# A fused decoder layer on one core: v projected from plain codes in four quarters, sine products swapped across partitions by transfers, and a new order of the four engines' lists

## The chip, the cores and the metric

The kernel runs on one core of one Trainium2 chip. The metric is device time in microseconds (us), the median of three runs. The engines are PE (TensorE, matrix products), DVE (VectorE), ACT (ScalarE), POOL (GpSimd) and SP (SyncE, which here only issues transfers). Each has its own list of instructions, written out by hand, and runs it in order; semaphores tie the lists together.

## What is computed

The reference takes x (128 sequences of 32 tokens, width 512) and computes, cut to what matters:

```
h = grouped_conv9(x) + context + bias
q, k, v = h @ Wq, h @ Wk, h @ Wv          # W = (codes - 8) * scale, one scale per 128 rows and column
q, k = rope(q), rope(k)                   # re = xe*cos - xo*sin ; ro = xo*cos + xe*sin
x = x + softmax(q k^T / sqrt(128) + causal) v @ Wo      # 32 query heads, 8 key/value heads of width 128
y = per-sequence 32x32 mixing of x (weights from a small network)
x = x + y @ Wbase^T + top-2-of-28 rank-8 LoRA experts(y)
```

## The kernel before

**Stages.** A setup block loads x, convolves it and leaves the hidden rows transposed in SBUF as two fp16 parts, high and low (`hT`). The attention block then runs 64 steps: 8 key/value heads (`g`) times 8 chunks of 512 tokens (`ch`). The last step runs into a tail that mixes the tokens and does the expert layer over 32 tiles of 128 tokens.

**A step.** Four query heads share one key/value head. Their projections fill PSUM banks 0 to 3 (`project_q(n, tile, kt)`), one matmul pair (high and low part of h) of 512 columns for each quarter `kt` of the width. The weights are plain codes, exact in fp16; between two quarters ACT multiplies the bank by a ratio of scales (`scale_q`), so that the sum ends in units of the last scale. The last scale is folded into the rope tables `rope_q` and `rope_k`. k does the same in bank 7 (`kv_bank`), scaled by DVE (`scale_k`). In the output projection ACT scales banks 4 and 5 (`scale_o`), and DVE adds the sum to `accT` (`add_out`).

v is different: its scales lie along the free axis. POOL multiplies its weights out once a head (`make_f`, `make_v_high`, `make_v_low`) and keeps a high and a low fp16 part. `project_v` therefore takes three passes (high by high, high by low, low by high) of four quarters for each of four token groups, 48 matmuls of 128 columns, in two halves; then ACT copies bank 7 to `v_f` (`move_v`) and POOL splits it (`v_high`, `v_low`).

**Rope.** DVE multiplies two banks at a time by the cosine (`turn_cos`, 128 partitions by 1024) and by the sine (`turn_sin`). The sine product of one half of the partitions belongs to the other half, so `turn_sin` writes across: two instructions of 64 partitions. POOL adds the two (`add_q`). Tiles 0 and 1 are pair 0, tiles 2 and 3 are pair 1. For k, POOL does all of it (`rotate_k_sin`, `rotate_k_cos`, `add_k`).

**Softmax.** `scores` makes 32 small matmuls onto the mask in bank 6; DVE transposes them and takes the maximum, POOL subtracts it (`shift`), ACT takes the exponential, DVE the sum and its inverse, POOL normalizes, DVE transposes back, POOL splits into two fp16 parts (`p_high`, `p_low`). `values` multiplies by v, and `out_high` (ACT) and `out_low` (DVE) split the result for the output projection.

**Pipeline.** One `body(n, i, p, r)` of each list works on four steps at once: the projections of n, the scores of i = n - 1, the values and most of the output of p = n - 2, and the end of the output of r = n - 3. Pair 0 of step n is turned at the end of body n; pair 1 is turned at the start of the next body, when it is step i. Before the change PE's body is: q(n,0,0), output(r,2,3), first half of v(i), q(n,0,1), values(p), second half of v(i), q(n,0,2), q(n,3,0), q(n,1,0), k(n,0), and then projections and output quarters in turn, with the scores in their midst. DVE's is: cosine of pair 1, add_out 2 and 3 of r, sine of pair 1, low halves 3, 1, 2, 0, mask, two scalings of k, scores transpose, maximum, third scaling of k, add_out 1 and 0, sum, inverse, cosine of pair 0 of n, transpose of the probabilities, sine of pair 0.

SP loads the codes of the next head in five pieces of 512 KB into two buffers, each when POOL has emptied one (`load_piece`), and the head's v scales.

Of the kernel before, what the change touches and what calls it, by code (L numbers as in the profile page):

```python
# [38 lines left out]
WSCALE = 256.0  # L39
# [11 lines left out]
class Rows:  # L51
# [28 lines left out]
class HeadWeights:  # L80
# [3 lines left out]
    def __init__(self, nc, c):  # L84
# [6 lines left out]
        self.k = sb("w_k", [P, 2, WKV // 2], F16)  # L91
        self.v = sb("w_v", [P, 2, 2, WKV // 2], F16)
# [3 lines left out]
        self.v_s = sb("v_s", [P, WKV // 2])  # L96
        self.f = sb("w_f", [P, WKV // 2])
# [10 lines left out]
        self.v_s_loaded = sem("v_s_loaded")  # L108
        self.piece_done = sem("piece_done")
        self.step = sem("w_step")  # L110

    def load_piece(self, sp, a, g, j):
# [7 lines left out]
        if j == 0:  # L120
            sp.dma_start(self.v_s[:], a["v_scales"][g].partition_broadcast(P)).then_inc(self.v_s_loaded, 16)
# [4 lines left out]
    def make_k(self, pool, g):  # L126
        self.wait_piece(pool, g, 0)
        pool.tensor_scalar(self.k[:, g % 2], self.codes[:, 0, 0:KT * HD], -8.0, 1.0, ALU.add, ALU.mult)

    def make_f(self, pool, g):  # L130
        pool.tensor_scalar(self.f[:], self.codes[:, 0, KT * HD:], -8.0, WSCALE, ALU.add, ALU.mult).then_inc(self.piece_done, 1)

    def make_v_high(self, pool, g):
        pool.wait_ge(self.v_s_loaded, 16 * (g + 1))
        pool.wait_ge(self.piece_done, PIECES * g + 1)
        pool.tensor_tensor(self.f[:], self.f[:], self.v_s[:], ALU.mult).then_inc(self.step, 1)
        pool.wait_ge(self.step, 2 * g + 1)
# [22 lines left out]
def prepare_and_convolve(nc, c, a, bank, accT, hT, w, rows):  # L160
# [39 lines left out]
    agg_hl = sb("agg_hl", [P, 2, S * S], F16)  # L200
    f_src = sb("f_src", [P, 2, 512])
# [28 lines left out]
    scale_step = sem("scale_step")  # L230
    conv_psum = sem("conv_psum")
# [26 lines left out]
    def _(sp):  # L258
# [51 lines left out]
    def _(pe):  # L310
# [61 lines left out]
        for n in range(2 * UNITS):  # L372
# [19 lines left out]
    def _(dve):  # L392
# [52 lines left out]

        def agg_lows(m):
# [16 lines left out]
        for n in range(2 * UNITS):  # L463
# [55 lines left out]
def attention_and_ffn(nc, c, a, banks, accT, hT, w, rows, out):  # L519
# [25 lines left out]
    q_sin = sb("q_sin", [P, 2, CHUNK])  # L545
    k_f = sb("k_f", [P, 2, CHUNK])
# [14 lines left out]
    v_psum = sem("v_psum")  # L561
    scores_psum = sem("scores_psum")
# [10 lines left out]
    q_sin_done = sems("q_sin_done", 2)  # L573
    q_ready = sems("q_ready", 2)
# [31 lines left out]
    lora = w.f[:, 0:2 * ER].rearrange("p (n e) -> p n e", n=2)  # L606
    loraT = w.v[0:EH, 0].rearrange("p a n -> p (a n)").rearrange("p (n l h t) -> p n l h t", n=2, l=2, h=2)
# [5 lines left out]
    gates = sb("gates", [P, 2, 2, EXPERTS])  # L613
# [79 lines left out]
    def _(sp):  # L693
        for g in range(1, NKV):
            for j in range(PIECES):
                w.load_piece(sp, a, g, j)


        def wait_chunk(ch):
# [4 lines left out]
            sp.wait_ge(v_psum, STEPS - CHUNKS + ch + 1)  # L704
# [10 lines left out]

        sp.dma_start(iota[:], a["iota"].partition_broadcast(P)).then_inc(iota_loaded, 16)
        wait_chunk(0)
        sp.dma_start(base, rows.base).then_inc(base_loaded, 16)
        wait_chunk(1)
        sp.dma_start(gl, rows.gl).then_inc(gl_loaded, 16)  # L720
        sp.dma_start(lb, rows.lb).then_inc(lb_loaded, 16)
        sp.wait_ge(mixw_zeroed, 2)
        for h in range(2):
# [3 lines left out]
        wait_chunk(5)  # L727
        sp.dma_start(aggb, rows.aggb.rearrange("b s -> (b s)").partition_broadcast(P)).then_inc(aggb_loaded, 16)
# [17 lines left out]
    def _(pe):  # L746
        def project_q(n, tile, kt):
            if kt:
                pe.wait_ge(q_scaled[tile], 3 * at(n) + kt)
            else:  # L750
                if n[1] == 0 and n[0]:
                    pe.wait_ge(w_ready, n[0])
                if at(n) and tile in (0, 3):

                    pe.wait_ge(q_sin_done[tile // 2], at(n))
                    pe.wait_ge(q_cos_done[tile // 2], at(n))
# [8 lines left out]
        def project_k(n, kt):  # L765
# [8 lines left out]
            for hp in range(2):  # L774
                mm = pe.matmul(kv_bank, w.k[:, n[2], kt * HD:(kt + 1) * HD], hT[:, n[1], kt, hp],  # L775
# [1001 lines left out]
```

## Time and profile before

| | |
|---|---|
| median of 3 runs (lowest, highest) | 1615.27 us (1615.13, 1615.29) |
| profiled execution: its time, its span | 1617.53 us, 1615.7 us |
| instructions | 36744 |
| PE busy | 1597.1 us, 99% |
| weight loads (overlap PE) | 894.6 us, 55% |
| DVE busy | 1399.0 us, 87% |
| ACT busy | 1231.1 us, 76% |
| POOL busy | 1127.9 us, 70% |
| transfers | 60.77 MB, 38 GB/s on average |
| granted TensorE clock | 0.997 |

The span is the profiled execution from its first to its last instruction. Busy time is a union over an engine's instructions; the ends of matmuls are modelled, and PE's pipelined matmuls overlap in it. An engine that waits in a semaphore is not busy. A mean duration of an instruction is longer than the time it takes of a full list where the next one starts before it has ended.

### The profile page before, as it was taken

What the parts mean: (1) busy time and instruction counts of PE and PEld (TensorE: products, weight loads), DVE (VectorE), ACT (ScalarE), POOL (GpSimd) and SP (SyncE); (2) the same over time, 40 slices, a digit from 0 to 9 for tenths busy, and PEclk for the clock granted to TensorE, in tenths of its full rate; (3) what the DMA queues carried; (4) which work ended last, traced back from release to release, by engine and by line L of the source; (5) the groups of instructions that cost most, each with busy time, mean ns of one, the idle gap of its engine ahead of it and who ended that gap; (6) DMA issues with size and microseconds to landing.
All of it is one profiled execution on the core that took longest, in us unless ns stands there. A gap on an engine that the chain in (4) does not pass through costs nothing.

```text
span 1615.7 us, 36744 instructions
## 1 busy us (share of the span) xinstructions
PE 1597.1 (99%) x14878; PEld 894.6 (55%) x14878; DVE 1399.0 (87%) x2176; ACT 1231.1 (76%) x2158; POOL 1127.9 (70%) x942
## 2 busy tenths in 40 slices
PE   9989999999999999999999999999999999899999
PEld 8845555555555555555555555555555555566665
DVE  5868888888888888888888888888888888888887
ACT  3458888888888888888888888888888888532222
POOL 1168877877787778777877787778787787623332
PEclk9999999999999999999999999999999999999999
DMA  8400010001000100010001000100000012122221
GB/s 303 136 25 15 14 34 15 14 15 34 15 14 14 34 14 15 14 34 14 14 15 34 14 15 15 34 14 15 15 2 28 26 11 83 34 72 80 79 82 50
DMA packets 32312, 60.77 MB, mean 38 GB/s; under 512 B 11512, under 2 KB 14392, under 8 KB 31888
## 3 DMA queue, kind: packets, MB, share of 16 engines
q1 hardware_dynamic: 32144, 58.42, 11.3%
q8 instruction: 119, 1.95, 0.5%
q14 instruction: 49, 0.40, 0.1%
HBM read 47.46 MB, written 10.95 MB: 36 GB/s over the span
## 4 chain that ended last, share of the span: by engine, by line
PE 92%; DVE 2%; POOL 1%; issue 0%; ACT 0%; POOLq 0%; DVEq 0%
PE banks L844 27%; PE banks L761 27%; PE banks L786 11%; PE banks L775 7%; PE banks L900 5%; PE banks L804 4%; PE banks L828 3%; PE banks L943 2%; PE banks L885 2%; PE banks L871 1%; PE banks L858 1%; POOL q_f L1408 1%; DVE q_sin L1136 0%; PE banks L934 0%; POOL k_f L1392 0%
## 5 line engine op out<-in xcount | busy, mean ns | idle before, releaser
L1530 ACT ACTIVATE banks<-banks,ratios 128x512 f32<-128x512 f32 x768 | 495.4, 676 | 119.9 <-PE banks L761 110.2
L761 PE MATMUL banks<-hT,w_q 128*128 128x512 f16 x2048 | 571.3, 380 | 7.4 <-DVE q_sin L1136 3.6
L844 PE MATMUL banks<-o_hl,w_o 128*128 128x512 f16 x2048 | 567.4, 379 | 0.6 <-DVE accT L1198 0.6
L1540 ACT ACTIVATE banks<-banks,ratios 128x512 f32<-128x512 f32 x768 | 479.4, 670 | 35.1 <-PE banks L844 35.0
L1408 POOL TENSOR_TENSOR q_f<-q_f,q_sin 128x1024 f32<-128x1024 f32 x128 | 301.7, 2357 | 68.6 <-DVE q_sin L1136 59.1
L844 PEld LDWEIGHTS banks<-o_hl,w_o 128*128 128x128 f16 x2048 | 187.0, 98 | 245.5 <-ACT banks L1540 50.4
L1136 DVE TENSOR_TENSOR q_sin<-banks,rope_q 64x1024 f32<-64x1024 f32 x256 | 312.8, 1222 | 8.1 <-POOL q_f L1408 2.4
L761 PEld LDWEIGHTS banks<-hT,w_q 128*128 128x128 f16 x2048 | 184.7, 98 | 236.0 <-DVE q_sin L1136 22.7
L786 PE MATMUL banks<-w_v,hT 128*128 128x128 f16 x3072 | 196.1, 221 | 0.0
L1129 DVE TENSOR_SCALAR banks<-banks,ratios 128x512 f32<-128x512 f32 x192 | 145.2, 756 | 56.7 <-PE banks L775 56.7
L786 PEld LDWEIGHTS banks<-w_v,hT 128*128 128x128 f16 x3072 | 180.1, 99 | 22.1 <-issue 0.7
L1392 POOL TENSOR_TENSOR k_f<-k_f,rope_k 64x512 f32<-64x512 f32 x128 | 162.3, 1268 | 14.5 <-POOL q_f L1408 10.7
L1198 DVE SCALAR_TENSOR_TENSOR accT<-banks,scales,accT 128x512 f32<-128x512 f32 x224 | 157.6, 745 | 9.4 <-PE banks L844 3.8
L1189 DVE TENSOR_TENSOR o_hl<-banks,o_hl 128x512 f16<-128x512 f32 x256 | 159.2, 684 | 2.9 <-ACT o_hl L1545 0.9
L1136 DVE TENSOR_TENSOR q_f<-banks,rope_q 128x1024 f32<-128x1024 f32 x128 | 154.1, 1204 | 3.6 <-PE banks L761 1.5
L775 PE MATMUL banks<-hT,w_k 128*128 128x512 f16 x512 | 152.8, 380 | 0.0
L1545 ACT ACTIVATE o_hl<-banks 128x512 f16<-128x512 f32 x256 | 132.3, 604 | 17.8 <-PE banks L828 17.8
L1412 POOL TENSOR_TENSOR sc<-sc,stats 128x512 f32<-128x512 f32 x64 | 67.0, 1047 | 103.3 <-DVE stats L1169 103.3
L1417 POOL TENSOR_TENSOR sc<-sc,stats 128x512 f32<-128x512 f32 x64 | 67.1, 1048 | 93.3 <-DVE stats L1177 93.3
L1156 DVE STREAM_TRANSPOSE sc<-banks 128x512 f32<-128x512 f32 x64 | 45.9, 717 | 74.4 <-PE banks L804 74.4
L1478 POOL TENSOR_TENSOR w_q<-hT,w_q 128x512 f16<-128x512 f32 x32 | 37.1, 1159 | 77.0 <-ACT w_q L1560 77.0
L900 PE MATMUL banks<-hT,w_o 128*128 128x512 f16 x372 | 85.4, 379 | 0.0
(131 smaller groups left out, 1930.0 us busy)
## 6 DMA issues: line engine op xcount, KB each, us to landing
codes<-in_codes SPq DMA_DIRECT2D x40, 512.0 KB, 3.7
accT<-in_xT SPq DMA_DIRECT2D x16, 512.0 KB, 9.7
hT<-in_x SPq DMA_DIRECT2D x32, 256.0 KB, 2.8
out<-codes SPq DMA_DIRECT2D x31, 256.0 KB, 2.0
v_s<-in_v_scales SPq DMA_DIRECT2D x8, 256.0 KB, 4.5
hT<-aggb_rows SPq DMA_DIRECT2D x1, 2048.0 KB, 7.1
f_src<-in_base_T SPq DMA_DIRECT2D x4, 256.0 KB, 9.6
base_rows<-f_hl SPq DMA_DIRECT2D x4, 256.0 KB, 3.2
```

The costliest lines, as they stand in the source:

```text
L761: mm = pe.matmul(banks[:, tile], w.q[:, n[2], kt * RF * HD + tile * HD:kt * RF * HD + (tile + 1) * HD], hT[:, n[1], kt, hp], start=kt == 0 ...
L775: mm = pe.matmul(kv_bank, w.k[:, n[2], kt * HD:(kt + 1) * HD], hT[:, n[1], kt, hp], start=kt == 0 and hp == 0, stop=hp == 1, skip_group_ch ...
L786: mm = pe.matmul(kv_bank[:, j * HD:(j + 1) * HD], hT[:, n[1], kt, hp, j * P:(j + 1) * P], w.v[:, n[2], wp, kt * HD:(kt + 1) * HD], start=m ...
L844: mm = pe.matmul(o_bank(tile), w.o[:, p[2], h * D + tile * P:h * D + (tile + 1) * P], o_hl[:, op, h], start=h == 0 and op == 0, stop=op == ...
L900: pe.matmul(base_bank(t), y_hl[:, t % 2, yp, k * P:(k + 1) * P], base[:, wp, k], start=i == 0, stop=False, skip_group_check=True)
L1136: return dve.tensor_tensor(dst.rearrange("p t (b s) -> p t b s", s=S), q, t, ALU.mult)
L1189: dve.tensor_tensor(lo, pv_bank(p, b).rearrange("p (j h q) -> p j h q", h=RF, q=S), hi, ALU.subtract).then_inc(out_ready[b], 1)
L1198: ins = dve.scalar_tensor_tensor(out=dst, in0=o_bank(tile), scalar=last, in1=dst, op0=ALU.mult, op1=ALU.add)
L1392: ins = pool.tensor_tensor(by_s(k_f[64 * h:64 * (h + 1), 1]), by_s(k_f[src, 0]), table(w.rope_k[:, n[2], 1], src), ALU.mult)
L1408: pool.tensor_tensor(q, q, q_sin[:], ALU.add).then_inc(q_ready[pair], 1)
L1530: act.activation(banks[:, tile], banks[:, tile], ACT.Copy, scale=w.ratios[:, n[0], tile, kt:kt + 1]).then_inc(q_scaled[tile], 1)
L1540: act.activation(o_bank(tile), o_bank(tile), ACT.Copy, scale=w.ratios[:, p[0], RF + tile, h:h + 1]).then_inc(o_scaled[tile], 1)
```

## The change

What it does, part by part:

- **v.** k and v now share one tensor of plain codes (`w.kv`), made by one POOL instruction a head. `project_v(n, kt)` does one quarter of the width at a time for all four token groups: 4 x 2 = 8 matmuls of 128 columns, 32 a step. After each quarter DVE multiplies bank 7 by a row of `v_table` (`scale_v`): the ratio of two scales, and after the last quarter the last scale, writing `v_f`. The table is made in the setup (six small DVE operations, one PE transpose, a store) and loaded once a head, broadcast over the partitions.
- **Sine.** `turn_sin` is one instruction of 128 partitions into `q_sin`. SP then issues two transfers of 64 partitions by 4 KB that put each half into the other half of a new buffer `q_sw` (`swap`), and `add_q` adds that. The sine waits until the previous swap has read `q_sin`, the swap until `add_q` of the other pair has read `q_sw`.
- **SP.** Its list is a body too: swap of pair 1 of i, loads of codes, table and tail data by chunk, swap of pair 0 of n.
- **Order.** Quarters 0 and 1 of v(n) lie at the end of body n, quarters 2 and 3 at the start of the next. Nothing of r is left in a body. New PE body: q(n,0,0), values(p), q(n,0,1), v(i,2), q(n,2,0), q(n,3,0), q(n,1,0), q(n,0,2), v(i,3), q(n,2,1), q(n,1,1), output(p,0,0), output(p,1,0), k(n,0), output(p,0,1), q(n,3,1), output(p,1,1), k(n,1), output(p,0,2), scores(i), output(p,1,2), output(p,0,3), k(n,2), q(n,1,2), output(p,1,3), q(n,0,3), output(p,2,0), k(n,3), q(n,1,3), output(p,3,0), output(p,2,1), v(n,0), output(p,3,1), q(n,2,2), output(p,2,2), v(n,1), output(p,3,2), q(n,3,2), output(p,2,3), output(p,3,3), q(n,2,3), q(n,3,3).
- New DVE body: cosine and sine of pair 1 of i, low half 3, scale_v(i,2), low halves 0, 2, 1, scale_v(i,3), mask, scale_k 0 and 1, scores transpose, maximum, add_out(p,0), scale_k 2, add_out(p,1), sum, inverse, sine of pair 0 of n, scale_v(n,0), cosine of pair 0, transpose of the probabilities, scale_v(n,1), add_out(p,2), add_out(p,3).
- New POOL body: rotate_k_cos(i), add_k(i), add_q(i,1), v_high, v_low, dequantize, shift, normalize, rotate_k_sin(n), p_high, p_low, add_q(n,0). ACT loses `move_v` and follows PE's new order.

The core of the diff:

```diff
+        def swap(n, pair):
+            sp.wait_ge(q_sin_done[pair], at(n) + 1)
+            if pair or at(n):
+                sp.wait_ge(q_ready[1 - pair], at(n) + pair)
+            for h in range(2):
+                sp.dma_start(q_sw[64 * h:64 * (h + 1)], q_sin[64 * (1 - h):64 * (2 - h)]).then_inc(q_swapped[pair], 16)
...
+        def load_weights(i):
+            g, ch, _ = i
+            if g + 1 < NKV:
+                if ch in (1, 3, 4):
+                    w.load_piece(sp, a, g + 1, {1: 2, 3: 3, 4: 4}[ch])
+                if ch == 2:
+                    if g:
+                        sp.wait_ge(v_moved, CHUNKS * g)
+                    w.load_v_table(sp, rows, g + 1)
+            if g + 2 < NKV and ch in (5, 6):
+                w.load_piece(sp, a, g + 2, 6 - ch)
...
-        def project_v(n, half):
-            if half == 0:
+        def project_v(n, kt):
+            if kt:
+                pe.wait_ge(v_scaled, 3 * at(n) + kt)
+            else:
                 pe.wait_ge(k_moved, at(n) + 1)
-            for j in (2 * half, 2 * half + 1):
-                m = 0
-                for kt in range(KT):
-                    for hp, wp in PASSES:
-                        mm = pe.matmul(kv_bank[:, j * HD:(j + 1) * HD], hT[:, n[1], kt, hp, j * P:(j + 1) * P],
-                                       w.v[:, n[2], wp, kt * HD:(kt + 1) * HD], start=m == 0, stop=m == 3 * KT - 1)
-                        m += 1
-            if half:
-                mm.then_inc(v_psum, 1)
+            for j in range(CT):
+                for hp in range(2):
+                    mm = pe.matmul(kv_bank[:, j * HD:(j + 1) * HD], hT[:, n[1], kt, hp, j * P:(j + 1) * P],
+                                   w.kv[:, n[2], (KT + kt) * HD:(KT + kt + 1) * HD], start=kt == 0 and j == 0 and hp == 0,
+                                   stop=hp == 1, skip_group_check=True)
+            mm.then_inc(v_psum, 1)
...
         def turn_sin(n, pair):
+            wait_q(n, pair)
             if pair or at(n):
-                dve.wait_ge(q_ready[1 - pair], at(n) + pair)
-            for h in range(2):
-                ins = turn(n, pair, 1, slice(64 * (1 - h), 64 * (2 - h)), q_sin[64 * h:64 * (h + 1)])
-            ins.then_inc(q_sin_done[pair], 1)
+                dve.wait_ge(q_swapped[1 - pair], 32 * (at(n) + pair))
+            turn(n, pair, 1, q_sin[:]).then_inc(q_sin_done[pair], 1)
+
+        def scale_v(n, kt):
+            dve.wait_ge(v_psum, KT * at(n) + kt + 1)
+            if n[1] == 0 and kt == 0:
+                dve.wait_ge(w.v_table_loaded, 16 * (n[0] + 1))
+            v = kv_bank.rearrange("p (j d) -> p j d", d=HD)
+            table = w.v_table[:, n[2], kt].unsqueeze(1).broadcast_to([P, CT, HD])
+            if kt < KT - 1:
+                dve.tensor_tensor(v, v, table, ALU.mult).then_inc(v_scaled, 1)
+            else:
+                if at(n):
+                    dve.wait_ge(v_ready, at(n))
+                dve.tensor_tensor(v_f[:], v, table, ALU.mult).then_inc(v_moved, 1)
...
         def add_q(n, pair):
-            pool.wait_ge(q_sin_done[pair], at(n) + 1)
-            if pair:
-                pool.wait_ge(k_sin_done, at(n) + 1)
+            pool.wait_ge(q_swapped[pair], 32 * (at(n) + 1))
+            pool.wait_ge(q_cos_done[pair], at(n) + 1)
+            if at(n) == 0 and pair == 0:
+                pool.wait_ge(k_sin_done, 1)
             q = q_f[:, 2 * pair:2 * pair + 2]
-            pool.tensor_tensor(q, q, q_sin[:], ALU.add).then_inc(q_ready[pair], 1)
+            pool.tensor_tensor(q, q, q_sw[:], ALU.add).then_inc(q_ready[pair], 1)
```

## Rows read from the trace of the kernel before

**Rows 1.** One line's instructions: ACT's move of k, once a step.

```profile
L1536 ACT ACTIVATE k_f<-banks x64: 589/628/634, 84.0 to 1375.6; 128x512 f32<-128x512 f32 x64
```

**Rows 2.** Groups by line and form: line, engine, tiles, forms, count | busy us, mean ns | idle before.

```profile
L1530 ACT ACTIVATE banks<-banks,ratios 128x512 f32<-128x512 f32 x768 | 495.4, 676 | 119.9 <-PE banks L761 110.2
...
L1136 DVE TENSOR_TENSOR q_sin<-banks,rope_q 64x1024 f32<-64x1024 f32 x256 | 312.8, 1222 | 8.1 <-POOL q_f L1408 2.4
L1408 POOL TENSOR_TENSOR q_f<-q_f,q_sin 128x1024 f32<-128x1024 f32 x128 | 301.7, 2357 | 68.6 <-DVE q_sin L1136 59.1 <-POOL k_f L1392 0.4
...
L1392 POOL TENSOR_TENSOR k_f<-k_f,rope_k 64x512 f32<-64x512 f32 x128 | 162.3, 1268 | 14.5 <-POOL q_f L1408 10.7
...
L1129 DVE TENSOR_SCALAR banks<-banks,ratios 128x512 f32<-128x512 f32 x192 | 145.2, 756 | 56.7 <-PE banks L775 56.7
...
L1440 POOL TENSOR_TENSOR pT_hl<-pT,pT_hl 128x512 f16<-128x512 f32 x64 | 74.0, 1156 | 5.1
...
L1417 POOL TENSOR_TENSOR sc<-sc,stats 128x512 f32<-128x512 f32 x64 | 67.1, 1048 | 93.3 <-DVE stats L1177 93.3
...
L1425 POOL CAST pT_hl<-pT 128x512 f16<-128x512 f32 x64 | 38.9, 608 | 0.0
```

**Rows 3.** Timeline of PE in one step: start, length, engine, line, tiles, count.

```profile
703.99 0.85 PE L828 MATMUL banks<-pT_hl,v_hl 32*128 32x128 f16 x48
...
704.78 1.51 PE L786 MATMUL banks<-w_v,hT 128*128 128x128 f16 x24
...
706.13 1.51 PE L761 MATMUL banks<-hT,w_q 128*128 128x512 f16 x6
...
711.57 1.08 PE L804 MATMUL banks<-q_f,k_f 128*32 128x128 f32 x32
...
712.59 1.04 PE L844 MATMUL banks<-o_hl,w_o 128*128 128x512 f16 x4
...
713.46 0.59 PE L775 MATMUL banks<-hT,w_k 128*128 128x512 f16 x2
```

**Rows 4.** The same timeline, DVE's instructions.

```profile
701.23 1.23 DVE L1136 TENSOR_TENSOR q_f<-banks,rope_q 128x1024 f32<-128x1024 f32 x1
...
702.37 1.40 DVE L1198 SCALAR_TENSOR_TENSOR accT<-banks,scales,accT 128x512 f32<-128x512 f32 x2
...
706.29 2.48 DVE L1189 TENSOR_TENSOR o_hl<-banks,o_hl 128x512 f16<-128x512 f32 x4
...
708.69 0.68 DVE L1165 CAST banks<-mask_b 128x512 f32<-128x512 bf16 x1
...
712.72 0.72 DVE L1156 STREAM_TRANSPOSE sc<-banks 128x512 f32<-128x512 f32 x1 [1.14 <-PE banks L804]
...
713.47 0.69 DVE L1169 TENSOR_REDUCE stats<-sc 128x16 f32<-128x512 f32 x1
...
714.96 1.41 DVE L1198 SCALAR_TENSOR_TENSOR accT<-banks,scales,accT 128x512 f32<-128x512 f32 x2
...
716.28 0.68 DVE L1173 TENSOR_REDUCE stats<-sc 128x16 f32<-128x512 f32 x1
...
717.16 1.18 DVE L1136 TENSOR_TENSOR q_f<-banks,rope_q 128x1024 f32<-128x1024 f32 x1
...
721.63 1.23 DVE L1136 TENSOR_TENSOR q_f<-banks,rope_q 128x1024 f32<-128x1024 f32 x1
```

**Rows 5.** Transfers by issue: tiles, queue, count, KB each, median us to landing.

```profile
codes<-in_codes SPq DMA_DIRECT2D x40, 512.0 KB, 3.7
...
out<-codes SPq DMA_DIRECT2D x31, 256.0 KB, 2.0
v_s<-in_v_scales SPq DMA_DIRECT2D x8, 256.0 KB, 4.5
```

**Rows 6.** Timeline of SP in the tail: two issues one behind the other.

```profile
1502.54 0.34 SPq L714 DMA_DIRECT2D out<-codes  x1
1502.92 0.43 SPq L710 DMA_DIRECT2D hT<-in_x  x1
```

More of the change, by code:

```diff
@@ L726, in _, with body @@
                              rows.aggw[:, h].rearrange("(t b) (i o) -> b i t o", b=TB, i=S)[b]).then_inc(mixw_loaded, 16)
-        wait_chunk(5)
-        sp.dma_start(aggb, rows.aggb.rearrange("b s -> (b s)").partition_broadcast(P)).then_inc(aggb_loaded, 16)
+        w.load_v_table(sp, rows, 0)
+        for j in range(2):
+            w.load_piece(sp, a, 1, j)
+        def body(n, i, p, r):
+            if i:
+                swap(i, 1)
+            if i:
+                load_weights(i)
+                load_ffn(i)
+            if n:
+                swap(n, 0)
+        swap(FIRST, 0)
+        program(body)
+        swap(LAST, 1)
         wait_chunk(6)
@@ L836, in output @@
             else:
-                if tile == (1 if p not in (PRIOR, LAST) else 0):
-                    for b in (0, 2, 1, 3):
+                if tile == 0:
+                    for b in (1, 2, 0, 3):
                         pe.wait_ge(out_ready[b], at(p) + 1)
@@ L979, in body @@
                 output(p, 1, 2)
-                output(p, 0, 2)
+                output(p, 0, 3)
             if n:
@@ L996, in body @@
             if n:
-                project_q(n, 2, 2)
+                project_k(n, 3)
+                project_q(n, 1, 3)
+            if p:
+                output(p, 3, 0)
+                output(p, 2, 1)
+            if n:
+                project_v(n, 0)
             if p:
@@ L1129, in scale_k, with turn, wait_q @@
             dve.tensor_scalar(kv_bank, kv_bank, w.ratios[:, n[0], K_ROW, kt:kt + 1], None, ALU.mult).then_inc(k_scaled, 1)
[L1131 to L1135 removed]
+        def turn(n, pair, which, dst):
+            t = w.rope_q[:, n[2], which, 2 * pair:2 * pair + 2].unsqueeze(2).broadcast_to([P, 2, CHUNK // S, S])
+            q = banks[:, 2 * pair:2 * pair + 2].rearrange("p t (b s) -> p t b s", s=S)
             return dve.tensor_tensor(dst.rearrange("p t (b s) -> p t b s", s=S), q, t, ALU.mult)
[L1138 to L1139 removed]
+        def wait_q(n, pair):
+            for tile in ((1, 0), (3, 2))[pair]:
                 dve.wait_ge(q_psum[tile], KT * at(n) + KT)
@@ L1287, in body @@
                 softmax_max(i)
+            if p:
+                add_out(p, 0)
             if n:
@@ L1296, in body @@
             if n:
+                turn_sin(n, 0)
+                scale_v(n, 0)
                 turn_cos(n, 0)
@@ L1300, in body @@
             if n:
-                turn_sin(n, 0)
+                scale_v(n, 1)
+            if p:
+                add_out(p, 2)
+                add_out(p, 3)
         scale_k(FIRST, 0)
```

335 lines of the change are left out of this document (176 added, 159 removed).

## The prediction

> **What bounds the kernel now.** I read the busy shares of the page first (the table above): PE 99%, DVE 87%, ACT 76%, POOL 70%. Such shares are averages, and PE's matmul ends are modelled, so I went on to one step of the attention loop. The row of line 1536 gives the beat: 64 steps, from 84.0 to 1375.6 us [rows 1], 20.5 us apart on average; the steady beat is that of DVE's cosine product, from 701.23 to 721.63, 20.4 us [rows 4]. So some 1265 of 1615.7 us are 62 equal beats, and the change is worth 62 times what it does to one.
>
> What PE does in a beat, from its timeline [rows 3]: between 712.59 and 713.46 four 512-column matmuls start, so a pair (one projection or output quarter) takes 0.432; 24 matmuls of v take 706.13 - 704.78 = 1.35, or 0.056 each; the values 704.78 - 703.99 = 0.79; the scores 712.59 - 711.57 = 1.02. A step has 36 pairs (16 of q, 4 of k, 16 of the output), 48 v matmuls, values, scores: 15.55 + 2.70 + 0.79 + 1.02 = 20.06. PE thus loses only 0.35 of 20.41 to waiting.
>
> DVE's timeline [rows 4] shows that it is bound too, in one half of the beat. From the transpose of the scores at 712.72 (1.15 after their first matmul) to the next cosine product at 721.63 it hardly pauses: 8.9 us; from 701.23 to the scores at 711.57 it is PE's list that runs out, 10.34 us. 10.34 + 1.15 + 8.91 = 20.40. The two halves meet in both engines, so a gain on one comes through only as far as the other allows. That is the sum to make for the new order.
>
> **The change on PE.** v takes plain codes, two passes instead of three: 32 matmuls of 128 columns for 48. 16 x 0.056 = 0.90 us a step goes; a quarter (8 matmuls) takes 0.45. PE's work is 19.16 a step.
>
> **The change on DVE.** Each sine product is two instructions of 64 partitions, 1222 ns each [rows 2]. One of 128 partitions is the shape of the cosine product: 1.23 long, and the next instruction starts 702.37 - 701.23 = 1.14 later [rows 4]. Twice a step, 4 x 1.22 - 2 x 1.14 = 2.60 goes. Four scalings of v by the table come, 128x512, PSUM times SBUF. The trace has no such instruction. Nearest below: the low halves of the output (PSUM and SBUF in, 128x512), four in 708.69 - 706.29, 0.60 each [rows 4]; nearest above: k's scaling, PSUM to PSUM, 0.756 [rows 2], with no overlap into the next. I take 0.60, since the 0.756 has a scale read per partition, which here is not there. So +2.40, between 2.40 and 3.02. DVE's total hardly moves; what counts is where it lies.
>
> **The beat of the new order.** Let S be the first matmul of scores(i). DVE's half, by starts [rows 4]: transpose at 1.15, +0.75 (713.47 - 712.72) maximum, +0.62 (its 0.69 less the usual overlap) add_out(0) at 2.52, +0.66 (716.28 - 714.96, halved) scale_k at 3.18, +0.67 add_out(1) at 3.85, +0.66 sum at 4.51, +0.88 (717.16 - 716.28, sum and inverse) sine of n at 5.39, +1.14 scale_v at 6.53, +0.60 cosine at 7.13, +1.14 transpose of the probabilities at 8.27, +0.72 scale_v at 8.99, +0.60 and twice 0.66, next cosine at 10.91. Against 10.06 (1.15 + 8.91) before: two scalings and both add_out of tiles 2 and 3 now lie in this half, one half sine less.
>
> PE's list in that half is the scores, 20 pairs, 2 quarters of v: 1.02 + 8.64 + 0.90 = 10.56, and its last q pair starts at 10.13. A pair ends 0.59 after its start [rows 3], a hop between engines costs about 0.06 (711.57 + 1.08 to 712.72, rows 3 and 4 together), so the cosine may start at 10.78, plus some 0.1 lost where ACT's scaling (0.676, [rows 2]) of an output tile has only three pairs of cover: 10.9. Both engines arrive together.
>
> The other half: the next cosine 1.14, its sine 1.23 to the end, hop 0.06: at 2.43 the banks of tiles 2 and 3 come free and PE, which has done q(0,0), the values, q(0,1) and a quarter of v by 2.1 after its own start, has waited some 0.4. From there 14 pairs and one quarter to the scores: 6.05 + 0.45 = 6.50. Around output(0,0), which waits for low halves 3, a v scaling, 0, 2, 1 behind the sine (2.38 + 5 x 0.60 + 0.08 + 0.06 = 5.5 against PE's 5.47), and at output(0,1) another 0.1. Half: 9.03. Beat: 10.91 + 9.03 = 19.94; I take 19.97, as three more things arrive within 0.1 of their need.
>
> One of them is POOL. k's sine halves, 2 x 1.27, now stand between normalize (1.05) and p_high (0.61), p_low (1.16) [rows 2]. Inverse ends 5.47, normalize 6.6, k's sine 9.2, p_low 11.06; the values of the next body start at 11.1. No slack, no loss.
>
> **The transfers.** Each sine product crosses the partitions by two transfers of 256 KB from SP. SP's issues stand 1502.92 - 1502.54 = 0.38 apart, 0.43 long [rows 6]; a 256 KB store out of SBUF lands 2.0 after its issue, a 512 KB load 3.7 [rows 5]. So both land after 0.4 + 2.0 = 2.4 at least, 0.4 + 3.7 = 4.1 at most; I take 2.7, nearer the store, since source and size are its own. Pair 1: sine ends at 2.4 after the cosine; add_q(n,0) on POOL, which frees the buffer, ends about then (11.06 + 2.36 = 13.4 after S, cosine at 10.9); hop, 2.7, add_q 2.36 [rows 2], hop: 7.8 against scores at 9.0. k_cos and add_k (two of 1.27) are done meanwhile. Cover 1.2: it holds to a landing of 3.9. Pair 0's has more. Codes and the v table are queued on SP behind the swap of pair 1, one a step, and nothing ahead of it waits: every wait of load_weights is for work of an earlier body.
>
> The trace's store and load bracket the landing with no rule needed. The Trainium skill ("DMA: Bandwidth & Descriptors", Anatomy of one DMA) gives about 2.0 us fixed, most of it the write's receipt, plus bytes over 436 GB/s, fitted on GpSimd's path; by it the 512 KB of a swap take an estimated 3.2 us. The sum would be the same 19.97 with 0.7 us of cover left in place of 1.2; it speaks for the slow case below, not for another likeliest one.
>
> **Other parts.** POOL's v weights (f, high, low) go, once a head, off the path: nothing. ACT loses one 0.6 copy: nothing, it idles. The v table in the setup: six small DVE operations, one transpose, one store of 16 KB under PE's convolution; if uncovered, under 2 us once. Before the last step's scores the same shorter lists apply: about -1.
>
> **Sum.** (20.41 - 19.97) x 62 = 27; with the end, -28. The profiled execution was 1617.5 with a span of 1615.7, 2.3 over the median of 1615.27; by medians 1587.
>
> **Rivals.** (1) PE alone sets the beat: the DVE half shrinks (its operations overlap better, or PE's wait for the sine is filled): 20.41 - 0.90 = 19.51, 1559. For: PE waits 0.35 only today. Against: the 10.91 above leaves it no room. (2) The scalings cost 0.756 without overlap, sines 1.22: 2 x 0.16 + 0.1 in DVE's half, 0.16 + 0.1 in the other's chain of low halves: +0.6 at most, beat 20.2 to 20.5, 1602 to 1621, most likely 1612: gains eaten. For: PSUM to PSUM is the dearer form in the trace. (3) Slower, by one mechanism: the swap lands late. Over 3.9 each microsecond is one on the beat; break-even at 3.9 + 0.44 = 4.35; at 5.0 the beat is 21.1 and the time 1655. For: the v scales' 256 KB took 4.5 behind a load [rows 5], and every step has two swaps. Against: the store's 2.0. (4) PE never notices v at all because DVE still sets 20.4: excluded by the shorter first half, save through (2).
>
> **How the numbers follow.** Forecast 0.53 (1579 to 1597); (1) 0.10; (2) 0.20; (3) 0.15; anything else 0.02. Below 1568 I leave some 0.05, over 1618 0.15 of (3) and a little of (2): range 1568 to 1618. A change under 0.2% (3.2 us) cannot be told. Faster: 0.53 + 0.10 + 0.13 of (2) = 0.77; same 0.06; slower 0.17.
>
> **What would show it.** The beat (line of k's move) at 19.9 to 20.0; 32 v matmuls a step at 0.056; the sine at about 1.2 for 128x1024, starting 1.14 behind the cosine; v's scaling under 0.70; q_sw landing 2.4 to 3.2 after the first issue, and scores not waiting for POOL's q_f; a PE wait of about 0.4 on q_sin and DVE without a gap from the scores' transpose to the cosine. It is wrong if scores wait for q_f (3), if a v scaling shows 0.75 (2), or if DVE has gaps in that half (1).

## The result and the profile after

The new kernel takes 1639.07 us (four runs, 1638.68 to 1639.18) against 1615.28 (1615.13 to 1616.33): a ratio of 1.0145, interval 1.0128 to 1.0163. It is slower by 23.8 us, where 28 less was forecast. The profiled execution took 1639.18 with a span of 1637.4, so the terms below are made against the forecast's span, 1615.7 - 28 = 1587.7: a miss of 49.7.

The first lines of the page after. Every engine is busy for less time than before, in a longer span:

```profile
span 1637.4 us, 35390 instructions
...
PE 1581.3 (97%) x13854; PEld 837.4 (51%) x13855; DVE 1373.0 (84%) x2311; ACT 1209.4 (74%) x2094; POOL 1105.3 (68%) x910
```

The line of k's move, after, answers to [rows 1]. 63 distances, 20.70 on average, where before had 20.50:

```profile
L1632 ACT ACTIVATE k_f<-banks x64: 578/587/597, 84.6 to 1388.4; 128x512 f32<-128x512 f32 x64
```

They aren't all alike. Of the first 62 distances from one step's scores to the next, 28 lie between 20.55 and 20.8, 20 are shorter, down to 20.34, and 14 are longer, up to 21.6. A step like the one shown next takes 20.69 to 20.70, which is called the steady beat below.

The groups by line and form, after, answer to [rows 2]. The operations came out as priced; the new thing is what stands at the end of the first line:

```profile
L1506 POOL TENSOR_TENSOR q_f<-q_f,q_sw 128x1024 f32<-128x1024 f32 x128 | 301.1, 2352 | 127.3 <-DMA q_sw<-q_sin 127.3
...
L1209 DVE TENSOR_TENSOR q_sin<-banks,rope_q 128x1024 f32<-128x1024 f32 x128 | 152.6, 1193 | 2.0 <-PE banks L829 1.4 <-DMA q_sw<-q_sin 0.6
...
L1236 DVE TENSOR_TENSOR banks<-banks,v_table 128x512 f32<-128x512 f32 x192 | 130.9, 682 | 2.0 <-PE banks L854 2.0
```

The waits of all engines, after (us in total, times, longest): `add_q` waits for the swap, and the scores' weight loads wait for `add_q`.

```profile
POOL q_f L1506 <- DMA q_sw<-q_sin: 127.3, 70, 2.9
...
PEld banks L871 <- POOL q_f L1506: 39.6, 62, 1.6
```

One step in the timeline, after. DVE, answering to [rows 4]: the transpose of one step's scores, the cosine and sine of pair 1, the transpose of the next step's scores.

```profile
700.02 0.72 DVE L1244 STREAM_TRANSPOSE sc<-banks 128x512 f32<-128x512 f32 x1 [0.83 <-PE banks L871]
...
709.81 1.23 DVE L1209 TENSOR_TENSOR q_f<-banks,rope_q 128x1024 f32<-128x1024 f32 x1
710.95 1.22 DVE L1209 TENSOR_TENSOR q_sin<-banks,rope_q 128x1024 f32<-128x1024 f32 x1
...
720.72 0.72 DVE L1244 STREAM_TRANSPOSE sc<-banks 128x512 f32<-128x512 f32 x1 [0.84 <-PE banks L871]
```

PE, answering to [rows 3]: the values with a wait ahead of them, and the scores.

```profile
708.75 1.46 PE L829 MATMUL banks<-hT,w_q 128*128 128x512 f16 x6
710.60 0.85 PE L896 MATMUL banks<-pT_hl,v_hl 32*128 32x128 f16 x48 [0.40 <-issue]
...
718.92 0.59 PE L912 MATMUL banks<-o_hl,w_o 128*128 128x512 f16 x2
719.57 1.08 PE L871 MATMUL banks<-q_f,k_f 128*32 128x128 f32 x32
```

POOL, from the dequantizing of codes (L132) and shift (L1510) over normalize (L1515) to `add_q(i,1)`:

```profile
700.70 1.04 POOL L132 TENSOR_SCALAR w_o<-codes 128x1024 f16<-128x1024 int32 x1
701.82 1.05 POOL L1510 TENSOR_TENSOR sc<-sc,stats 128x512 f32<-128x512 f32 x1
704.62 1.05 POOL L1515 TENSOR_TENSOR sc<-sc,stats 128x512 f32<-128x512 f32 x1 [1.75 <-DVE stats L1265]
705.84 2.59 POOL L1489 TENSOR_TENSOR k_f<-k_f,rope_k 64x512 f32<-64x512 f32 x2 [0.17 <-POOL sc L1515]
708.55 0.61 POOL L1525 CAST pT_hl<-pT 128x512 f16<-128x512 f32 x1
709.24 1.16 POOL L1540 TENSOR_TENSOR pT_hl<-pT,pT_hl 128x512 f16<-128x512 f32 x1
710.35 2.36 POOL L1506 TENSOR_TENSOR q_f<-q_f,q_sw 128x1024 f32<-128x1024 f32 x1
...
714.02 1.26 POOL L1498 TENSOR_TENSOR k_f<-k_f 128x512 f32<-128x512 f32 x1
717.17 2.35 POOL L1506 TENSOR_TENSOR q_f<-q_f,q_sw 128x1024 f32<-128x1024 f32 x1 [1.89 <-DMA q_sw<-q_sin]
```

SP in that step:

```profile
712.78 1.10 SPq L740 DMA_DIRECT2D q_sw<-q_sin  x2
```

**The chain in these rows.** Pair 1's sine ends at 710.95 + 1.22 = 712.17. The buffer `q_sw` is free only when `add_q` of pair 0 ends, at 710.35 + 2.36 = 712.71; SP issues at 712.78. `add_q(i,1)` starts at 717.17, 4.39 after the issue, ends at 719.52, and the scores start at 719.57. POOL has been idle for 1.89, as k's `add_k` was done at 715.28. From cosine to scores: 719.57 - 709.81 = 9.76, against a forecast of 9.03. The other half came as forecast: scores start 1.15 ahead of their transpose, so at 698.87, and 709.81 - 698.87 = 10.94 against 10.91. 10.94 + 9.76 = 20.70.

### The profile page after: what moved, and what is told of

Its sections match the earlier page's. It is cut to its first block and busy times, and to the rows that moved or that the text cites. A ratio compares the mean times of both kernels' runs of the same rounds, so it can differ in the third digit from the quotient of the medians.

```text
span 1637.4 us, 35390 instructions
## 1 busy us (share of the span) xinstructions
PE 1581.3 (97%) x13854; PEld 837.4 (51%) x13855; DVE 1373.0 (84%) x2311; ACT 1209.4 (74%) x2094; POOL 1105.3 (68%) x910
## 5 line engine op out<-in xcount | busy, mean ns | idle before, releaser
L1506 POOL TENSOR_TENSOR q_f<-q_f,q_sw 128x1024 f32<-128x1024 f32 x128 | 301.1, 2352 | 127.3 <-DMA q_sw<-q_sin 127.3
L829 PEld LDWEIGHTS banks<-hT,w_q 128*128 128x128 f16 x2048 | 175.5, 97 | 249.6 <-ACT banks L1626 67.7
L912 PEld LDWEIGHTS banks<-o_hl,w_o 128*128 128x128 f16 x2048 | 176.5, 98 | 238.4 <-ACT banks L1636 73.0
L854 PEld LDWEIGHTS banks<-w_kv,hT 128*128 128x128 f16 x2048 | 133.4, 98 | 67.4 <-ACT k_f L1632 14.5
L854 PE MATMUL banks<-w_kv,hT 128*128 128x128 f16 x2048 | 157.4, 220 | 2.5 <-DVE banks L1236 2.0
L1209 DVE TENSOR_TENSOR q_sin<-banks,rope_q 128x1024 f32<-128x1024 f32 x128 | 152.6, 1193 | 2.0 <-PE banks L829 1.4
L843 PE MATMUL banks<-hT,w_kv 128*128 128x512 f16 x512 | 152.3, 379 | 1.2 <-DVE banks L1203 1.2
L1515 POOL TENSOR_TENSOR sc<-sc,stats 128x512 f32<-128x512 f32 x64 | 67.1, 1048 | 111.3 <-DVE stats L1265 111.3
L1236 DVE TENSOR_TENSOR banks<-banks,v_table 128x512 f32<-128x512 f32 x192 | 130.9, 682 | 2.0 <-PE banks L854 2.0
```

What stands on the lines that cost most here:

```text
L829: mm = pe.matmul(banks[:, tile], w.q[:, n[2], kt * RF * HD + tile * HD:kt * RF * HD + (tile + 1) * HD], hT[:, n[1], kt, hp], start=kt == 0 ...
L843: mm = pe.matmul(kv_bank, w.kv[:, n[2], kt * HD:(kt + 1) * HD], hT[:, n[1], kt, hp], start=kt == 0 and hp == 0, stop=hp == 1, skip_group_c ...
L854: mm = pe.matmul(kv_bank[:, j * HD:(j + 1) * HD], hT[:, n[1], kt, hp, j * P:(j + 1) * P], w.kv[:, n[2], (KT + kt) * HD:(KT + kt + 1) * HD] ...
L912: mm = pe.matmul(o_bank(tile), w.o[:, p[2], h * D + tile * P:h * D + (tile + 1) * P], o_hl[:, op, h], start=h == 0 and op == 0, stop=op == ...
L1209: return dve.tensor_tensor(dst.rearrange("p t (b s) -> p t b s", s=S), q, t, ALU.mult)
L1506: pool.tensor_tensor(q, q, q_sw[:], ALU.add).then_inc(q_ready[pair], 1)
```

## The experiments

Each ratio below is against the kernel before, run beside the experiment (medians 1615.67 to 1616.79 us).

First theory A: the swap's latency sets the beat. First rival B: the latency is hidden, and the new order itself (POOL's list, the sine behind the cosine) sets it.

**e1, no transfer, one buffer.** `add_q` reads `q_sin` itself. Left out: the sine product isn't crossed between the halves.

```diff
-            sp.wait_ge(q_sin_done[pair], at(n) + 1)
-            if pair or at(n):
-                sp.wait_ge(q_ready[1 - pair], at(n) + pair)
-            for h in range(2):
-                sp.dma_start(q_sw[64 * h:64 * (h + 1)], q_sin[64 * (1 - h):64 * (2 - h)]).then_inc(q_swapped[pair], 16)
+            return
...
-                dve.wait_ge(q_swapped[1 - pair], 32 * (at(n) + pair))
+                dve.wait_ge(q_ready[1 - pair], at(n) + pair)
...
-            pool.tensor_tensor(q, q, q_sw[:], ALU.add).then_inc(q_ready[pair], 1)
+            pool.tensor_tensor(q, q, q_sin[:], ALU.add).then_inc(q_ready[pair], 1)
```

> The new kernel without its swaps: POOL adds the sine product straight from q_sin (so each half of the partitions gets its own sine product and not the other's; this part of the computation is changed), and DVE's next sine waits for that addition. Order, v and all else stay. Theory A (the swaps' latency sets the beat: cosine, sine, 0.5 us for the buffer, 4.3 us of transfer, 2.35 of add_q, then the scores): the scores no longer wait for q_f, the beat falls from 20.7 to the 19.97 of the prediction, and the time by 62 x 0.7 = 45 us, to about 1594. Theory B (the new order and the scalings of v on DVE cost the time, transfers or not): the beat stays above 20.5 and the time above 1627. Theory C (transfers slow other engines by their traffic): instructions on DVE and POOL get shorter.

Measured: 1707.76 us, ratio 1.0565 (1.0548 to 1.0583). Theories A and C missed, and B's "above 1627" was met for a reason that none of them names. The row of DVE's timeline of e1 says why:

```profile
720.11 1.22 DVE L1205 TENSOR_TENSOR q_sin<-banks,rope_q 128x1024 f32<-128x1024 f32 x1 [1.65 <-POOL q_f L1502]
```

With one tile in place of two, the sine of pair 1 waits until POOL has added pair 0. The experiment took away a transfer and a buffer at once, and says nothing of the transfer by itself. What it does show is that the swap is also the second buffer of this order.

**e2, two buffers for the swap.** `q_sw` gets a half for each pair; room comes from one v table in place of two and from the probabilities sharing `v_f`.

```diff
-            if pair or at(n):
-                sp.wait_ge(q_ready[1 - pair], at(n) + pair)
+            if at(n):
+                sp.wait_ge(q_ready[pair], at(n))
```

> Two buffers q_sw, one for each pair, so that a swap no longer waits for the addition of the other pair (room comes from pT sharing v_f's memory and one v table buffer, loaded in chunk 7). Theory A: the 0.5 us between the end of pair 1's sine and its first issue goes; the chain cosine 1.14, sine 1.22, transfer 4.3, add_q 2.35 is then 9.1 long, about PE's own 9.03, so the beat is 20.1 to 20.2 and the time 1639 - 62 x 0.55 = about 1605. If the wait were not on the path: no change.

Measured: 1622.88 us, ratio 1.0038 (1.0026 to 1.0051), steady beat 20.35. With the 0.6 us wait for the buffer gone, 16 us come back, about half of what was expected (1605 us).

**e3, two buffers, and the sine of pair 1 ahead of its cosine.** e2 with this:

```diff
-                turn_cos(i, 1)
                 turn_sin(i, 1)
+                turn_cos(i, 1)
```

> The two buffers of e2_two_buffers, and pair 1's sine ahead of its cosine (the reverse of the order that the change chose). Theory A: the transfer starts 1.14 us earlier and is covered with about 1 us to spare; PE alone and DVE set the beat, 19.97 to 20.05, the time is 1594 to 1600, as without transfers. Theory B: no better than e2_two_buffers, above 1620.

Measured: 1618.38 us, ratio 1.0014 (1.0004 to 1.0023). The swap starts 1.14 earlier and the scores stand 1.37 behind `add_q(i,1)`: they don't wait for it. Yet the steady beat is e2's, 20.35, where 19.97 to 20.05 was expected; the 4.5 us come from the steps with a late landing. Something else holds 20.35, and theory A explains only what lies above it. Rows of e3 (POOL's shift, normalize and `p_low`; PE's scores and values):

```profile
712.01 1.05 POOL L1508 TENSOR_TENSOR sc<-sc,stats 128x512 f32<-128x512 f32 x1 [1.18 <-DVE stats L1257]
...
714.86 1.05 POOL L1513 TENSOR_TENSOR sc<-sc,stats 128x512 f32<-128x512 f32 x1 [1.81 <-DVE stats L1265]
...
719.48 1.16 POOL L1538 TENSOR_TENSOR pT_hl<-v_f,pT_hl 128x512 f16<-128x512 f32 x1
```
```profile
709.34 1.08 PE L871 MATMUL banks<-q_f,k_f 128*32 128x128 f32 x32
...
720.84 0.85 PE L896 MATMUL banks<-pT_hl,v_hl 32*128 32x128 f16 x48 [0.24 <-issue]
```

Counted from the scores, shift starts at 2.67, normalize at 5.52, `p_low` ends at 11.30, and the values start at 11.50 after a wait of 0.24.

**e4, crossed by DVE, one buffer.** e1 with the two 64-partition instructions of the kernel before.

```diff
-            turn(n, pair, 1, q_sin[:]).then_inc(q_sin_done[pair], 1)
+            for h in range(2):
+                src = slice(64 * (1 - h), 64 * (2 - h))
+                t = w.rope_q[src, n[2], 1, 2 * pair:2 * pair + 2].unsqueeze(2).broadcast_to([64, 2, CHUNK // S, S])
+                q = banks[src, 2 * pair:2 * pair + 2].rearrange("p t (b s) -> p t b s", s=S)
+                ins = dve.tensor_tensor(q_sin[64 * h:64 * (h + 1)].rearrange("p t (b s) -> p t b s", s=S), q, t, ALU.mult)
+            ins.then_inc(q_sin_done[pair], 1)
```

> The sine swap alone undone: DVE writes the sine product across in two instructions of 64 partitions, as before the change, no transfers; v by quarters and the new order stay. DVE gains 1.3 us in each half of the beat. If DVE's list between the scores' transpose and the next cosine is the path, as the prediction has it, the beat is 10.94 + 1.3 + 10.3 = about 22.5 and the time 1639 + 62 x 1.8 = about 1750; if DVE has slack there (theory B's reading that PE or ACT waits elsewhere), it stays within 10 us of 1639.

Measured: 1928.61 us, ratio 1.1939 (1.1917 to 1.1961), where 1750 was expected. The coupling of e1 again, with longer sines, and PE waits long enough to be granted half its clock once in most steps (mean clock 0.953 for the span). It too was confounded by the buffer.

**e6 and e7, the same two with two buffers for `q_sin`.** They repair e1 and e4 (the edit is shown against e1):

```diff
-            if pair or at(n):
-                dve.wait_ge(q_ready[1 - pair], at(n) + pair)
-            turn(n, pair, 1, q_sin[:]).then_inc(q_sin_done[pair], 1)
+            if at(n):
+                dve.wait_ge(q_ready[pair], at(n))
+            turn(n, pair, 1, q_sin2[:, pair]).then_inc(q_sin_done[pair], 1)
```

In e6 the sine product isn't crossed; e7 crosses it with the two DVE instructions of e4.

> The new order, cosine of pair 1 first, no transfers: two sine buffers, add_q reads them directly (each half of the partitions gets its own sine product; this part of the computation is changed). Unlike in e1_no_transfer no sine waits for the addition of the other pair. If the transfers cost by their latency alone, and e1_no_transfer was slow only through that shared buffer, this is the beat of e3_sine_first where nothing lands late: 20.35, time 1612 to 1618. If transfers also slow the engines by their traffic, it is faster than that. If the new order is bad in itself: above 1630.

> e6_no_transfer_two_buffers with DVE writing the sine across in two halves, as before the change: computes the full layer without transfers. DVE takes 1.3 us more in each half of the beat. Expected 20.35 + 2.4 to 2.6, a beat of 22.8 and about 1765 us, if DVE's list is the path in both halves; near 1616 if DVE has slack. Either way its distance to e2_two_buffers is what the transfers save.

Measured: e6 1615.06 us, ratio 0.9988 (0.9978 to 0.9997), steady beat 20.35; e7 1763.43, ratio 1.0914 (1.0896 to 1.0932), beat 22.7, where 22.8 was expected. With no transfer at all the beat is again 20.35, and `add_q(i,1)` is done 1.85 before the scores: so in the steady beat the transfers cost by their latency alone. And in the new order, crossing on DVE costs 1763 - 1623 = 140 us more than the swap of e2, as two instructions of 1222 ns stand for one of about that length twice a step in DVE's full list. The new order stands on the swap.

**e5, k's sine in two parts.** e3, with one half of k's sine on POOL moved behind `p_low`. Theory C, formed on e3: POOL's list from normalize to `p_low` holds 20.35.

```diff
             if n:
-                rotate_k_sin(n)
+                rotate_k_sin(n, (0,))
...
             if n:
+                rotate_k_sin(n, (1,))
                 add_q(n, 0)
```

> e3_sine_first with POOL's second half of k's sine behind p_low in place of ahead of p_high. In e3_sine_first the beat is 20.35, the values start 0.4 us late behind p_low, and ACT's list, late by as much, delays four products of the next half. Theory A (POOL's k sine ahead of p_high and p_low, a near tie in the prediction, is what is left): p_low ends about 0.5 us earlier, the values start when PE comes to them, the beat falls to the predicted 19.97 to 20.05 and the time by some 20 us, to 1595 to 1600. Theory B (what is left lies in DVE's list or ACT's own): the beat stays at 20.3 and the time at 1616 to 1618.

Measured: 1601.87 us, ratio 0.9923 (0.9901 to 0.9945), span 1599.0. POOL's timeline of e5:

```profile
706.80 1.05 POOL L1515 TENSOR_TENSOR sc<-sc,stats 128x512 f32<-128x512 f32 x1 [1.80 <-DVE stats L1266]
708.02 1.27 POOL L1490 TENSOR_TENSOR k_f<-k_f,rope_k 64x512 f32<-64x512 f32 x1 [0.17 <-POOL sc L1515]
710.21 0.61 POOL L1525 CAST pT_hl<-v_f 128x512 f16<-128x512 f32 x1 [0.92 <-DVE v_f L1271]
710.90 1.16 POOL L1540 TENSOR_TENSOR pT_hl<-v_f,pT_hl 128x512 f16<-128x512 f32 x1
712.23 1.26 POOL L1490 TENSOR_TENSOR k_f<-k_f,rope_k 64x512 f32<-64x512 f32 x1 [0.17 <-POOL pT_hl L1540]
```

and PE's, from one step's scores to the values:

```profile
701.28 1.08 PE L872 MATMUL banks<-q_f,k_f 128*32 128x128 f32 x32
...
712.47 0.85 PE L897 MATMUL banks<-pT_hl,v_hl 32*128 32x128 f16 x48
```

POOL now waits 0.92 for DVE's transpose ahead of `p_high`, so it has slack there, and the values stand 712.47 - 701.28 = 11.19 behind the scores with no wait. In the kernel after they stood 710.60 - 698.87 = 11.73 behind, with a wait of 0.40. The beat is 20.05, as expected (the median lies 2 us over the expected 1595 to 1600): theory C holds. So A and B each had a part: the swap held the beat above 20.35, and POOL's list in the new order held it there. This version is faster than both kernels.

**e8, idle products in the tail.** The clock was granted at half for some us around the last step, in e5 behind this wait of PE:

```profile
1362.19 1.89 PE L913 MATMUL banks<-o_hl,w_o 128*128 128x512 f16 x4 [3.88 <-DVE o_hl L1276]
```

e8 is e5 with 14 matmuls, whose result is not used, ahead of `output(PRIOR,0,0)`.

```diff
         project_v(LAST, 2)
+        pe.wait_ge(q_cos_done[0], STEPS)
+        pe.wait_ge(q_sin_done[0], STEPS)
+        for _ in range(14):
+            pe.matmul(banks[:, 0], w.kv[:, LAST[2], 0:HD], hT[:, LAST[1], 0, 0], start=True, stop=True)
         output(PRIOR, 0, 0)
```

> e5_split_k_sine with 14 matmuls of 512 columns into a free bank after project_v(LAST, 2), where PE otherwise idles 3.35 us before output(PRIOR, 0, 0) and the granted clock is 0.5 for the next 6.8 us. Theory: the idling costs the clock and so 3 to 5 us of the tail; with the products the clock stays at 1.0 there and the span from the last move of k to the end falls from 249 to about 245. Rival: the tail is long because of waits of ACT and POOL in the new order; then the clock stays up and the tail is still 249.

Measured: 1599.82 us, ratio 0.9905 (0.9888 to 0.9921). Windows of two stretches of the tail (the third number from the end is the granted clock), of e5:

```profile
1362.00:1366.00 4.00, 3.76 (x16) 1.81 (x17) 1.16 (x3) 1.53 (x3) 3.53 (x2) 0.57 0.63 227
1374.00:1379.00 5.00, 3.01 (x14) 1.88 (x15) 1.65 (x3) 2.96 (x6) 4.88 (x6) 0.68 0.01 2
```

and of e8:

```profile
1362.00:1366.00 4.00, 3.18 (x23) 1.73 (x22) 1.98 (x3) 2.58 (x5) 3.21 (x2) 1.00 0.90 298
1374.00:1379.00 5.00, 3.99 (x20) 2.49 (x21) 1.88 (x8) 1.82 (x4) 4.78 (x5) 0.66 0.00 2
```

The first slow stretch is gone, the second is not. The span is 1.2 us shorter, where 3 to 5 were expected: the last distance between scores falls from 21.95 to 20.70, and what lies behind the last scores stays as long (231.5, and 231.1 in e5). (The medians are 2.05 apart, but e5's four runs alone spread over 7.0.) So this stretch of the clock cost about 1 us; the rest of the tail was not taken apart.

**e9, straight halves; e10, one transfer; e12, even and odd partitions.** What makes the swap land late? All three are the kernel after with the issue changed, and in none does the sine product reach the right half (e9 and e10 copy straight, e12 exchanges neighbours).

```diff
 e9  sp.dma_start(q_sw[64 * h:64 * (h + 1)], q_sin[64 * h:64 * (h + 1)])     # h = 0, 1
 e10 sp.dma_start(q_sw[:], q_sin[:])
 e12 sp.dma_start(q_sw[h:P:2], q_sin[1 - h:P:2])                             # h = 0, 1
```

> The new kernel with its two transfers copying each half of the partitions to the same half and not across (the sine product stays on its own partitions; this part of the computation is changed). The swap's packets of 4 KB took about 0.30 us each in the new kernel against 0.159 in the codes' loads, and its data phase 2.3 us. Theory A: crossing partitions is what doubles the packets; then they take 0.16, the data phase 1.3, and the scores come 0.5 us or more earlier (beat 20.35, the next limit). Theory B: reading and writing SBUF in one transfer is what doubles them, whatever the partitions: packets 0.30, beat 20.7, no change of the time.

> The new kernel with one transfer of 512 KB over 128 partitions in place of the two (straight, so the sine product stays on its own partitions; this part of the computation is changed). If the second issue, 0.5 us behind the first, is on the path: landing falls from 4.3 to about 3.8 us after the sine's issue and the beat to 20.35. If the data phase of 2.3 us is what counts and starts with the first issue: no more than 0.2 us is saved, the beat is 20.5 to 20.7.

> The new kernel with its two transfers taking the odd partitions to the even ones and back, 64 partitions each as before but spread over all 128 (the sine product then crosses between neighbours and not between halves; this part of the computation is changed). Two transfers over one half each had packets of 0.28 us and a data phase of 2.3 us, crossed or not; one over all 128 had 0.16 and 1.4. If it is the side-by-side partitions of a half that halve the rate, packets fall to 0.16 to 0.2, the last ends 0.5 us or more earlier, the landing is 3.7 to 3.9 us after the first issue and the beat 20.35. If it is having two transfers of 64 rows, nothing changes: packets 0.28, beat 20.7.

Measured: e9 1641.35 us, ratio 1.0152 (1.0130 to 1.0174); e10 1616.45, ratio 1.0002 (0.9991 to 1.0012); e12 1616.46, ratio 1.0000 (0.9989 to 1.0012). Times to landing of each issue, in the order after, e9, e10, e12:

```profile
DMA to landing us min/median/max: 2.8/3.7/5.1
```
```profile
DMA to landing us min/median/max: 2.9/3.7/5.4
```
```profile
DMA to landing us min/median/max: 2.9/3.1/5.0
```
```profile
DMA to landing us min/median/max: 2.2/2.4/4.6
```

Windows from a swap's first packet to its last, of the same four, each in a step in which no load runs beside it (the last two numbers are the busy share of the 16 DMA engines and GB/s):

```profile
706.76:709.03 2.27, 2.27 (x17) 1.06 (x15) 2.27 (x4) 2.06 (x4) 2.09 (x3) 1.00 0.91 231
```
```profile
666.25:668.53 2.28, 2.28 (x17) 1.07 (x15) 2.28 (x4) 2.06 (x4) 2.10 (x3) 1.00 0.91 230
```
```profile
697.28:698.71 1.43, 1.43 (x15) 0.83 (x12) 1.43 (x3) 1.43 (x3) 1.37 (x2) 1.00 0.89 364
```
```profile
697.51:698.94 1.43, 1.43 (x15) 0.83 (x12) 1.43 (x3) 1.43 (x3) 1.37 (x2) 1.00 0.91 367
```

A packet is one partition's 4 KB, and a swap has 128. In the kernel after they take 0.91 x 2.27 x 16 = 33.1 us of engine time, 0.26 each; in e12 0.91 x 1.43 x 16 = 20.8, 0.16 each. So two transfers over 64 neighbouring partitions each move at 0.63 of the rate (231 of 367 GB/s), crossed (after) or straight (e9), and the same 64 packets over every second partition move at the full one. The crossing costs nothing. In pair 1's step `add_q` starts 3.24 after the issue in e10 and 3.01 in e12, against 4.39.

Another rival for the lateness is the 512 KB of codes that SP issues right behind the swap in five of eight steps. A step of the kernel after without them, SP and POOL:

```profile
589.10 1.10 SPq L740 DMA_DIRECT2D q_sw<-q_sin  x2
```
```profile
593.34 2.35 POOL L1506 TENSOR_TENSOR q_f<-q_f,q_sw 128x1024 f32<-128x1024 f32 x1 [1.74 <-DMA q_sw<-q_sin]
```

Here it starts 4.24 after the issue, against 4.38 to 4.40 with codes behind: the loads cost 0.15 of it.

In e10 and e12 the steady beat is 20.35 even with the one `q_sw`: the whole 0.34 comes back, as it did in e2 by the second buffer alone: either is enough to bring the swap below POOL's limit. Why neighbours are slow was not tested further.

**e11, the sine first, one buffer.** The order of e3 alone.

```diff
-                turn_cos(i, 1)
                 turn_sin(i, 1)
+                turn_cos(i, 1)
```

> The new kernel with one edit: pair 1's sine ahead of its cosine (the order that the title reverses), one buffer q_sw as it is. The sine ends 1.14 us earlier, but its swap then waits for add_q of pair 0 to free the buffer, which ends 0.5 us after the sine does now. So by theory A only what the buffer allows is gained: no more than 0.1, beat 20.6 to 20.7, time within 8 us of 1639. If the order alone were the fault, it would come down to the 20.35 of e3_sine_first, 1618.

Measured: 1638.13 us, ratio 1.0137 (1.0119 to 1.0155). A sine that is ready earlier is worth nothing while the swap waits for POOL to empty `q_sw`.

## Why the prediction was wrong, step by step

Beats and spans, as they fall when the causes are taken away one after another:

| kernel | what holds the beat | steady beat | span |
|---|---|---|---|
| after | swap of pair 1: buffer and landing | 20.69 | 1637.4 |
| e3 (and e2, e6, e10, e12) | POOL's list ahead of `p_low` | 20.35 | 1616.1 (e3) |
| e5 | not taken apart; neither POOL's list nor the swap | 20.05 | 1599.0 |
| forecast | | 19.97 | 1587.7 |

In e2, e6, e10 and e12, as in e3, `p_low` ends 11.30 and the values start 11.50 behind the scores in the steady steps.

- **The swap's price: the step that failed.** "I take 2.7, nearer the store, since source and size are its own", with "Cover 1.2: it holds to a landing of 3.9". In the step shown above `add_q` started 4.39 after the issue. The upper bound, 4.1, was too low as well. And "`add_q(n,0)` on POOL, which frees the buffer, ends about then": it ended 0.54 behind the sine, and the issue left 0.61 behind it. 2.36 + 0.61 + 4.39 + 2.35 + 0.05 = 9.76, the measured half. This is rival (3), which had 0.15; its form (each further microsecond is one on the beat) was right: in the step whose swap was issued at 838.14, `add_q` started 5.07 after the issue, 0.68 later, and the beat was 21.38, 0.69 longer. Undoing it gives 1637.4 - 1616.1 = 21.3 us of the 49.7.
- **Why 2.7 looked right.** The store of 256 KB with 2.0 goes over all 128 partitions; the swap's halves go over 64 neighbours each. e10 shows the price of the same bytes in one piece, 3.1 from its issue: over 2.7 too, but within the cover. By the Trainium skill ("DMA: Bandwidth & Descriptors", Anatomy of one DMA) the 512 KB take an estimated 3.2: e10 agrees with it, and the halves of the kernel after don't.
- **POOL: "No slack, no loss" failed.** Where the swap is in time (e3), normalize starts 5.52 behind the scores, as forecast (6.6 - 1.05 = 5.55). But `p_low` ends at 11.30, not 11.06: the sum of durations was about right, and each instruction that waits for the one ahead of it on the same engine starts 0.08 to 0.17 late (705.84 against 704.62 + 1.05). The values start another 0.20 later, at 11.50, where the forecast had 11.1 and where PE in e5 was ready at 11.19. That is 0.31, and the two beats are 0.30 apart. A tie with no slack in a sum of durations is a loss. Undoing it gives 1616.1 - 1599.0 = 17.1 us.
- **The two failures feed each other.** In the kernel after, the scores start just as the late `add_q(i,1)` ends, so POOL's splitting of v and the dequantizing of codes stand right ahead of shift. It starts 701.82 - 698.87 = 2.95 behind the scores instead of 2.67 (e3), normalize 704.62 - 698.87 = 5.75 instead of 5.52, and `p_low` ends at 11.53. POOL's lateness in turn is 0.44 of the 0.54 by which the buffer comes free behind the sine (712.71 - 698.87 = 13.84, against 13.4). Steps without codes to dequantize are the short ones, 20.34 to 20.5, unless a landing is late.
- **The rest, 11.3 us.** By the first and last scores: 97.54 to 1367.87 in e5 is 1270.3 where the forecast makes 1289.2 (before: 97.99 to 1387.19) - 28 = 1261.2, so 9 lie in the loop: 0.08 a beat in the steady beat (5), and steps with a late landing with the last, longer distance (4). "About -1" for the end was wrong in sign: the last distance is 21.95, against 21.59 before. e8 brings it to 20.70, so about 1 us of it is the clock. Another 2.6, which the forecast had at nothing, lie behind the last scores, 1599.0 - 1367.87 = 231.1 against 228.5 before; e8 doesn't change them, and their cause stays open.
- **What was right.** The first half, 10.91 against 10.94 (10.87 in e2, where the swap isn't late). PE's list without v's third pass. The sine at 1.19 long, 1.14 behind the cosine. The cost of v's scaling: I took 0.60 between 0.60 and 0.756; the instructions are 0.68 long, but the next starts 0.60 after (712.80 to 713.40). So rival (2) didn't happen, nor (1). SP's queue held nothing up: the swap's lateness is buffer and landing, but for the 0.15 of the codes. With both ties loosened the change as a whole gains: e5 is 1601.87 against 1615.28. What v's part gains by itself was not tried.

## What to carry to other kernels

Price a transfer that takes an instruction's place by one over the same partitions, not only of the same bytes, from the first issue to the start of its consumer, and list who frees each buffer and when: a second buffer was worth 16 us here, and one taken away unnoticed spoiled e1 and e4. Where a sum of durations ends in a tie, put the handovers between instructions of one engine in before calling it free. And look for the limit behind the first: they stood 0.34 and 0.30 us apart, and lifting the first alone only brought the time of before back.

## What the runs showed of the hardware that was not expected

- Two SBUF-to-SBUF transfers of 64 neighbouring partitions each move 230 to 231 GB/s with the DMA engines 0.91 busy; one over all 128, or two over every second one, move 364 to 367 GB/s at 0.89 to 0.91.
- Landing times scatter: the same issue takes 2.8 to 5.1 us in the kernel after, 2.2 to 4.6 even in e12. A cover that holds for the median still loses on some steps.
- In the tail of e5 PE was granted half its clock (0.57 over 1362 to 1366) behind a wait of 3.88 us, and again (0.68 over 1374 to 1379) around waits of 0.65, 1.08 and 1.17. In e8, when 14 unused products filled the first wait, it kept the full clock there (1.00), and not in the second place (0.66).
